# Layer-norm sums taken out of the residual additions and ScalarE squares, causal maxima by a fused VectorE instruction, rounding in one step, and new lists of the chains' order

## The reference

```python
x = x + L0_window_attention(layernorm(x))
x = x + L0_cross_attention(layernorm(x), ctx, ctx, mask)
x = x + L0_slots(layernorm(x))
x = x + L1_causal_attention(layernorm(x))      # softmax(q k / 4 + bias), bias holds the causal mask
x = x + L1_cross_attention(layernorm(x), ctx)
x = x + L1_mlp(layernorm(x))                   # quantized linear, depthwise conv, silu, quantized linear
```

## Time and profile before

| | |
|---|---|
| median of 3 executions | 3288.36 us (3285.29 to 3289.53) |
| the profiled execution | 3283.83 us, its span 3282.0 us |
| granted TensorE clock, mean of the span | 0.955 |
| PE busy (matmuls) | 2836.4 us, 86% |
| DVE (VectorE) busy | 2522.0 us, 77% |
| ACT (ScalarE) busy | 2178.7 us, 66% |
| POOL (GpSimd) busy | 755.3 us, 23% |
| DMA | 43.47 MB, mean 13 GB/s |

### The profile page before, as it was taken

The page is one execution under the profiler, slowest core; times in us unless marked ns, Lnnn a source line. Parts: engine busy times, 40 slices in busy tenths (PEclk is TensorE's granted clock), DMA queues, the critical chain, the costliest instruction groups (busy, mean ns, idle before and its releaser), DMA issues.

```text
span 3282.0 us, 59801 instructions
## 1 busy us (share of the span) xinstructions
PE 2836.4 (86%) x23406; PEld 2073.9 (63%) x23406; DVE 2522.0 (77%) x5446; ACT 2178.7 (66%) x4271; POOL 755.3 (23%) x1360
## 2 busy tenths in 40 slices
PE   3799986999878998899988998889988999889985
PEld 3566754676656766577666676567665676656763
DVE  6856599766898579975898769986799768987676
ACT  2368764678646876577855777657865687557773
POOL 1420013300233112330133112422032301232100
PEclk8799997999989999899999999999999999999996
DMA  5000010000000000000000000000000000000000
GB/s 157 1 1 1 4 27 17 1 1 5 24 12 9 1 16 12 20 1 1 16 21 11 1 4 13 24 9 1 5 24 12 9 1 16 16 17 1 1 1 13
DMA packets 43468, 43.47 MB, mean 13 GB/s; under 512 B 8577, under 2 KB 41185, under 8 KB 43185
## 3 DMA queue, kind: packets, MB, share of 16 engines
q1 hardware_dynamic: 41200, 36.46, 3.8%
q10 hardware_dynamic: 1984, 3.18, 0.3%
HBM read 31.24 MB, written 8.39 MB: 12 GB/s over the span
## 4 chain that ended last, share of the span: by engine, by line
PE 49%; DVE 31%; ACT 11%; POOL 4%; issue 4%; DMA 1%; SPq 0%; DVEq 0%; POOLq 0%; ACTq 0%
PE banks L1179 8%; PE banks L1213 7%; DVE chain_m L696 5%; PE banks L1322 4%; PE banks L1222 4%; PE banks L1260 4%; PE banks L1197 3%; DVE chain_arena L890 3%; PE banks L1286 2%; DVE chain_arena L927 2%; PE banks L1406 2%; DVE chain_arena L730 2%; DVE chain_arena L931 2%; DVE chain_stat L674 2%; DVE chain_arena L774 2%
## 5 line engine op out<-in xcount | busy, mean ns | idle before, releaser
L1213 PE MATMUL banks<-chain_arena 64*128 64x256 f32 x3072 | 426.2, 399 | 42.4 <-DVE chain_m L696 28.1
L696 DVE TENSOR_REDUCE chain_m<-banks 128x4 f32<-128x512 f32 x512 | 328.7, 681 | 84.8 <-PE banks L1213 84.2
L1515 POOL TENSOR_SCALAR chain_ng<-chain_sv 128x2 f32<-128x2 f32 x192 | 52.9, 276 | 1408.4 <-DVE chain_sv L677 1408.3
L1213 PEld LDWEIGHTS banks<-chain_arena 64*128 64x128 f32 x3072 | 286.0, 191 | 119.9 <-DVE chain_m L696 41.2
L1034 ACT ACTIVATE chain_arena<-chain_arena,chain_m 128x128 f32<-128x128 f32 x1024 | 324.1, 393 | 25.9 <-DVE chain_m L696 23.2
L968 ACT ACTIVATE chain_xn<-chain_xa,chain_nm,chain_rs 128x256 f32<-128x256 f32 x384 | 209.4, 596 | 166.3 <-POOL chain_nm L1519 165.5
L1260 PE MATMUL banks<-chain_arena 64*128 64x256 f32 x2048 | 268.2, 382 | 0.0
L692 DVE TENSOR_TENSOR chain_arena<-banks,pos_bias 128x512 f32<-128x512 f32 x256 | 174.9, 683 | 95.6 <-PE banks L1213 94.6
L1222 PE MATMUL banks<-chain_arena,chain_va 128*32 128x128 f32 x5120 | 198.1, 281 | 40.5 <-ACT chain_arena L1013 27.4
L1260 PEld LDWEIGHTS banks<-chain_arena 64*128 64x128 f32 x2048 | 200.5, 192 | 23.5
L1569 POOL TENSOR_TENSOR chain_arena<-chain_arena 128x512 f32<-128x512 f32 x128 | 169.5, 1341 | 148.4 <-DVE chain_arena L774 148.0
(11 more groups left out here) (314 smaller groups left out, 6979.1 us busy)
## 6 DMA issues: line engine op xcount, KB each, us to landing
chain_xn<-in_ctx SPq DMA_DIRECT2D x32, 256.0 KB, 2.8
chain_xa<-in_x SPq DMA_DIRECT2D x32, 256.0 KB, 3.1
out<-chain_xa SPq DMA_DIRECT2D x32, 256.0 KB, 2.2
chain_arena<-in_mask SPq DMA_DIRECT2D x32, 128.0 KB, 3.5
f_w1t<-in_w1t ACTq DMA_DIRECT2D x1, 1024.0 KB, 7.0
f_w2t<-in_w2t ACTq DMA_DIRECT2D x1, 1024.0 KB, 14.3
wqkv0T<-in_wqkv0T ACTq DMA_DIRECT2D x1, 768.0 KB, 16.8
whh<-in_whh SPq DMA_DIRECT2D x1, 768.0 KB, 10.3
```

Source lines behind the costliest of these rows:

```text
L696: e.tensor_reduce(m, s.rearrange("p (j o) t -> p j o t", o=2), AX.X, ALU.max, negate=True).then_inc(*done(f"{tag}_mx{u}"))
L1213: mm[i] = e.matmul(c.ps[:, i, 2 * T * j:2 * T * j + 2 * T], t["qh"][p, j, x, b, :], flat(t["kx"][p, j, b]), start=not masked, stop=not mas ...
```

## The change

The sums of the norms `b`, `f`, `1`, `x` and `g` no longer come from `bn_stats`. The residual addition before each becomes two `tensor_tensor_reduce` calls of 128x256 (`add_rows`), which also give the sum of each row. ScalarE turns it into the negated mean (128x2) and takes two `Square` activations of 128x256 with that mean as bias, whose accumulated output is the sum of squared differences. GpSimd makes variance plus epsilon from it, and the root and product as before. The norm `a`, of the input, stays as it was. In the causal attention each score tile takes four `tensor_tensor_reduce` calls of 128x128, which write `-(score + bias)` and the minimum of it, in place of one addition and one reduction; the exponential gets `scale=-1.0`. The hidden tile of the MLP is rounded by one VectorE instruction that adds and subtracts the constant. All lists of `ORDER` are new. The number of steps per turn falls from 85 to 80 on VectorE, rises from 81 to 84 on ScalarE, and stays on TensorE (92), GpSimd (17) and SyncE (2).

```diff
+def add_rows(e, c, tag, rows):
+    for b in range(B):
+        x = c.t["xa"][:, b, :]
+        y = e.tensor_tensor_reduce(x, rows(b), x, 1.0, 0.0, ALU.add, ALU.add, c.t["sm"][:, b:b + 1])
+    y.then_inc(*c.dve.now(f"{tag}_y"))
...
 def maxima_vector(e, c, n, tag, k, bias=False):
...
-            e.tensor_tensor(flat(t["s"][:, u % 4]), c.ps[:, u % 2, :], flat(k["pos_bias"][:, r]), ALU.add).then_inc(*done(f"{tag}_bi{u}"))
-            e.wait_ge(*dve(f"{tag}_bi{u}"))
-        s = t["s"][:, u % 4] if bias else bank(c, u % 2)
+            for a in range(PER):
+                mx = e.tensor_tensor_reduce(t["s"][:, u % 4, a], bank(c, u % 2)[:, a], k["pos_bias"][:, r, a // 2, a % 2], -1.0, 3e38, ALU.add, ALU.min,
+                                            max_of(t["m"], b, r, a))
+            mx.then_inc(*done(f"{tag}_mx{u}"))
+            yield
+            continue
+        s = bank(c, u % 2)
...
-    e.tensor_tensor(flat(t["xa"][:]), c.ps[:, 1, :], flat(t["xa"][:]), ALU.add).then_inc(*done(f"{tag}_y"))
+    add_rows(e, c, tag, lambda b: c.ps[:, 1, D * b:D * b + D])
...
-        e.wait_ge(*act(f"g_ro{b}"))
-        e.tensor_scalar(t["hq"][:, :, b, :], cv[:, :, b, :], -ROUND, None, ALU.add).then_inc(*done(f"g_r2{b}"))
+        e.wait_ge(*dve(f"g_mu{b}"))
+        e.tensor_scalar(t["hq"][:, :, b, :], cv[:, :, b, :], ROUND, -ROUND, ALU.add, ALU.add).then_inc(*done(f"g_r2{b}"))
...
-    yield from norm_vector(e, c, n, "b", "a_y")
-    yield from norm_vector(e, c, n, "f", "b_y")
-    yield from norm_vector(e, c, n, "1", "f_y")
-    yield from norm_vector(e, c, n, "x", "1_y")
-    yield from norm_vector(e, c, n, "g", "x_y")
...
-def norm_scalar(e, c, n, tag):
+def norm_scalar(e, c, n, tag, before=None):
+    if before:
+        e.wait_ge(*dve(f"{before}_y"))
+        e.activation(t["ng"][:], t["sm"][:], ACT.Copy, scale=-1.0 / D).then_inc(*done(f"{tag}_ng"))
+        e.wait_ge(*act(f"{tag}_ng"))
+        for b in range(B):
+            sq = e.activation(t["xn"][:, b, :], t["xa"][:, b, :], ACT.Square, bias=t["ng"][:, b:b + 1], accum_out=t["sq"][:, b:b + 1])
+        sq.then_inc(*done(f"{tag}_sq"))
+        yield
     e.wait_ge(*pool(f"{tag}_nm"))
...
-                ex = e.activation(s, s, ACT.Exp, bias=max_of(t["m"], u // GROUPS, row_group(u), a))
+                ex = e.activation(s, s, ACT.Exp, scale=-1.0, bias=max_of(t["m"], u // GROUPS, row_group(u), a))
...
-    for b in range(B):
-        v = t["cv"][:, :, b, :]
-        e.wait_ge(*dve(f"g_mu{b}"))
-        e.activation(v, v, ACT.Identity, bias=k["rounder"][:, 0:1]).then_inc(*done(f"g_ro{b}"))
...
 def norm_pool(e, c, n, tag, k):
+    else:
+        e.wait_ge(*act(f"{tag}_sq"))
+        e.tensor_scalar(t["rv"][:], t["sq"][:], 1.0 / D, LN_EPS, ALU.mult, ALU.add).then_inc(*done(f"{tag}_ve"))
+        e.wait_ge(*pool(f"{tag}_ve"))
```

Of the lists one line stands for all, the start of ScalarE's:

```diff
     "scalar": (
-        "301233030131230200313110223021122012333000121132233330303013...
+        "132011312312013033121223001302032021110133332102102102101331...
```

More of the change, by code:

```diff
@@ L100 @@
     "sync": (
[L101 removed]
+        "0011223313123020113322001133220011332200113322001133220011332200"),
     "pool": (
[L103 to L105 removed]
@@ new lines @@
+        "1320113322001320111133331120222300031202032103210320131321103320221110013333111122211323313323220200"
+        "1322012000300032012011130323311121022331113131013133300223232132222003021202000003021021031103233111"
+        "1201111223313103130033322321323222200102230200003020102103110323311112011112233131031300333223213232"
+        "2220010223020000302010210311032331111201111223313103130033322321323222200102230200003020102103110323"
+        "3111120111122331310313003332232132322220010223020000302010210311032331111201111223313103130033322321"
@@ L791, in window_vector @@
     e.wait_ge(*pe("a_pr"))
-    e.tensor_tensor(flat(t["xa"][:]), c.ps[:, 1, :], flat(t["xa"][:]), ALU.add).then_inc(*done("a_y"))
+    add_rows(e, c, "a", lambda b: c.ps[:, 1, D * b:D * b + D])
     yield
@@ L853, in slots_vector @@
     e.wait_ge(*pe("f_o"))
-    e.tensor_tensor(t["xa"][:], ps[:, :, 0:D], t["xa"][:], ALU.add).then_inc(*done("f_y"))
+    add_rows(e, c, "f", lambda b: ps[:, b, 0:D])
     yield
@@ L1075, in scalar_turn @@
     yield
-    yield from norm_scalar(e, c, n, "b")
+    yield from norm_scalar(e, c, n, "b", "a")
     e.wait_ge(*pe("b_T"))
@@ L1088, in scalar_turn @@
     yield from outputs_scalar(e, c, n, "b")
-    yield from norm_scalar(e, c, n, "f")
+    yield from norm_scalar(e, c, n, "f", "b")
     yield from normalized_scalar(e, c, n, "f", t["xnT"], 0)
@@ L1109, in scalar_turn @@
     yield
-    yield from norm_scalar(e, c, n, "1")
+    yield from norm_scalar(e, c, n, "1", "f")
     yield from normalized_scalar(e, c, n, "1", t["xnT"], 0)
@@ L1115, in scalar_turn @@
     yield from outputs_scalar(e, c, n, "1")
-    yield from norm_scalar(e, c, n, "x")
+    yield from norm_scalar(e, c, n, "x", "1")
     yield from normalized_scalar(e, c, n, "x", t["xnT"], 0)
@@ L1121, in scalar_turn @@
     yield from outputs_scalar(e, c, n, "x")
-    yield from norm_scalar(e, c, n, "g")
+    yield from norm_scalar(e, c, n, "g", "x")
     e.wait_ge(*dve("g_sc"))
@@ L1512, in norm_pool @@
 def norm_pool(e, c, n, tag, k):
-    t, dve, pool, done = c.t, c.dve.of(n), c.pool.of(n), c.pool.now
-    e.wait_ge(*dve(f"{tag}_mv1"))
-    e.tensor_scalar(t["ng"][:], t["sv"][:, :, 0], -1.0, None, ALU.mult).then_inc(*done(f"{tag}_ng"))
-    e.wait_ge(*dve(f"{tag}_ve"))
+    t, act, dve, pool, done = c.t, c.act.of(n), c.dve.of(n), c.pool.of(n), c.pool.now
+    if tag == "a":
+        e.wait_ge(*dve(f"{tag}_mv1"))
+        e.tensor_scalar(t["ng"][:], t["sv"][:, :, 0], -1.0, None, ALU.mult).then_inc(*done(f"{tag}_ng"))
+        e.wait_ge(*dve(f"{tag}_ve"))
+    else:
+        e.wait_ge(*act(f"{tag}_sq"))
+        e.tensor_scalar(t["rv"][:], t["sq"][:], 1.0 / D, LN_EPS, ALU.mult, ALU.add).then_inc(*done(f"{tag}_ve"))
+        e.wait_ge(*pool(f"{tag}_ve"))
     e.tensor_tensor(t["rs"][:], t["rv"][:], k["neg_half"][:], ALU.pow).then_inc(*done(f"{tag}_rs"))
```

213 lines of the change are left out of this document (101 added, 112 removed).

## The result

Slower: 3307.6 us, median of 4 runs (3304.1 to 3309.5), against 3289.0 for the kernel before on the same chip; ratio 1.0056, 95% interval 1.0039 to 1.0073. I had forecast 3261.

A forecast was written before the change was run, and what follows sets the result against it. No single engine bounds the kernel: VectorE sets the middle stretch of each 385.5 us period, TensorE the last. Terms -6.0 + 3.0 - 0.4 = -3.4 us per period, -27 in eight, took 3288.4 to 3261; range 3240 to 3282, chance 0.50.

The forecast's parts named there:

- +3.0 per period for ScalarE: First and last stretches of a period: ScalarE's free time falls from 56 to 41 us, lengthening TensorE's idle time by 3.
- The bounds reading: VectorE, 92% busy, sets the middle 142 us stretch; 7 norms saving 0.93 us each shorten it by 6.0 per period.
- VectorE's sum: VectorE's busy time over the run: norms -149 us, causal tiles +25, together -124 of 2522 (-233 to +153).
- the fused maxima give nothing: Causal tiles: four fused calls at 0.367 us make 1.47 against 1.37 now, +25 us over 256 tiles.
- ScalarE's sum: ScalarE's busy time: squares and means +206 us over 160 norms, 64 roundings gone -72, together +134 (to +200).
- Rounding: MLP hidden tile: the rounding chain without its ScalarE step gets shorter, counted as -0.4 us per period.
- I add nothing for the ends: Set-up, start and drain outside the eight periods (198 us): no change counted, though the lists differ there too.
- better lists: Rival: new lists mix the middle stretch with the others, cutting TensorE's idle time; -72 in all, 3216; chance 0.18.
- Half rate: Rival: the fused VectorE call's columns cost twice, 0.77 us per 256 and 0.50 per 128; +42, 3330; chance 0.08.
- The wash: Rival: ScalarE's extra visits in its strict list cancel the middle stretch's gain, within 6.6 us of 3288; chance 0.12.
- The longer way: Rival: norm path lengthens by 0.68 us, five times per turn, and sets the period; +34, 3322; chance 0.12.
- the three signs: Signs of error: 128-column call over 0.45 us, square much dearer than plain activation, ScalarE's product wait well above 166 us.

The follow-up runs named there:

- run 9: Kernel before, lists untouched, with a discarded negated mean and two squares on an always-ready tile added behind each of 160 pairs of normalized rows on ScalarE: 3426.4 us, +142.3.
- run 10: Kernel before plus one ScalarE turn per norm, a discarded 0.2 us instruction waiting for the residual addition; run 6 without its squares: 3345.8 us, +61.7.
- run 6: Kernel before with its own norm, plus ScalarE turns computing unused negated mean and squares, on the same ScalarE list as run 3: 3395.8 us, +109.8.
- run 5: Run 3 with each square over 8 of a row's 256 columns (variance not the reference's): 3345.3 us, +59.2 against the kernel before.
- run 3: Kernel before with the norm change alone, 160 turns put into ScalarE's list, 443 other turns shifted one to five places: 3376.3 us, +89.2.
- run 7: All three parts of the change, squares moved to the head of the normalized rows' turn, so no added turn and the order of before: 3598.8 us, +312.7.
- run 14: Kernel before, no instruction changed, lists searched anew: 3218.4 us, -65.7.
- run 15: Changed kernel, instructions unchanged, lists searched with the same effort as run 14: 3229.9 us, -54.2 against the kernel before.
- run 16: Kernel before on the lists of run 14, with only the causal tiles through the fused call: 3207.1 us, -78.7 against the kernel before.
- run 8: Changed kernel on its new lists with the old norm back and the added turns gone: 3349.0 us, +62.9 against the kernel before.
- run 12: Kernel before, no instruction touched, with run 3's ScalarE list minus the added turns (443 turns one to five places away): 3345.4 us, +57.0.
- run 18: Causal tiles and rounding as changed, norm as before, lists searched nearly twice as long as for run 15: 3169.2 us, -119.3 against the kernel before.

## Why the prediction was wrong

**The step that failed: +3.0 per period for ScalarE.** It let the squares lie in ScalarE's idle time, and made the price grow as that time shrinks. In the steady part TensorE's waits for ScalarE grew by 11.0 us per period and not by 3.0. Runs of its own bear it out: run 9 has +142 in all, some 18 per period, for 205 us of dead work with the lists untouched, and the squares alone are +48 (run 10 against 6). Busy 66% did not mean room. A microsecond of work on ScalarE came through at 0.3 to 0.7: 48 for 161 of busy time from run 10 to 6, 30 for 61 from run 5 to 3, 142 for 205 in run 9. What sets that factor was not isolated. That in a fixed order everything behind an instruction is late with it is argued from runs 7 and 9, where TensorE's waits for ScalarE grow by 190 and 109 us; a part comes through the granted clock, as the table shows.

**The bounds reading**, -6.0 per period, held that VectorE sets the middle stretch, so that work taken from it counts there almost in full. In the changed kernel TensorE's waits for VectorE fell by 7.7 per period, causal tiles included, so its size was about right there. It isn't a property of the instructions alone, as I took it to be: with the old lists the statistics of 160 norms came off VectorE and TensorE's waits for it stayed (226 and 228 us, runs 6 and 3). So the forecast -6.0 + 3.0 stands against -7.7 + 11.0, with 1.2 more for GpSimd, where I had put nothing, and 1.7 more of TensorE's busy time.

**Where the 19 us come from.** Runs 14 to 16 split them: with the lists of one search each, the changed instructions are 11.5 us slower (norm +24.5, causal tiles -13, rounding 0), and the new lists of the change stand 7 us further from what the search finds than the old ones (72.9 against 65.7). The norm's price was 25 to 37 with own lists, 32 in the steps on one list and 60 with the old list kept. It was a gain of 44 only on the lists made for it (run 8). The split between norm and lists is soft: it depends on two searches that need not be equally lucky, and a longer one moved run 15 by 24 us.

**VectorE's sum** was -124 us and is -283. I had put the read behind the call (0.082 more) and the call at its full length. Measured start to start, a call is 0.21 us at 128 columns (I took 0.367) and 0.34 at 256 (2028.27 to 2028.61; I took 0.50). A tile is 0.9, not 1.47. So "the fused maxima give nothing" was wrong by its price: they are what gains. The Trainium skill, "VectorE: DVE Perf Modes", section on two Vector instructions with no wait between them, says that an accumulator output is two instructions, and the trace agrees: 1024 reads beside 1024 calls. To add a time for the second was my step, and the timeline shows it covered by the next call.

**ScalarE's sum**, +134, is +109. The new instructions cost what I took: the squares with their reads are busy for 174.9 us, 0.547 each (I took 0.545), the means 32.9. The total grew by less than these make, since ScalarE's instructions overlap with their neighbours; I did not follow where. The size of the work was about right, its price in time was not.

**Rounding**, -0.4 per period: 0, within 6 us.

**"I add nothing for the ends"**: the steady part loses some 65 us and the rest gives some 45 back. I did not follow where in the ends.

**The lists.** I gave better lists 18 in 100 and no case to worse ones. Run 12 shows +57 from small shifts, runs 14 and 18 show 66 and more to be had. The order was the largest term of this kernel, and I had it only as a rival.

**The rivals and the signs.** Half rate is out. The wash is out: 18.7 is beyond 6.6. The longer way had the sign right, and as a mechanism it is not shown. The way grew, by 0.41 us at its shortest (I had said 0.68) and 0.87 in the mean, but the mean is as long with the old way kept (4.76 in run 6) and 4.47 with nothing changed but the list (run 12): so most of the lateness comes with ScalarE's order and load, and not with the longer chain of steps. The wait that I had named for it shrank. None of the three signs by which I wanted to know that I was wrong appeared (a call over 0.45 us, a dear square, a longer wait for the product). I had named none for plain work on ScalarE, which is what it was.

## What to carry to other kernels

Where several chains share engines in a fixed order, an engine's idle share is no room. Before moving work to the engine that everybody passes, try a dead copy of it there; it showed the sign here and overstated the size (142 us in run 9, 53 above its list in run 6, 25 to 37 for the norm change with own lists). Split TensorE's idle time by the engine it waits for, before and after: it told here in one table what the busy times did not. Moving work off the busier engine was worth less than its time, and less than what the receiver paid. When instructions change, compare each set with lists made for it by equal effort, and measure the list alone, since an order fitted to one set cost 44 us under another here (run 8).

## What the hardware showed unexpectedly

- VectorE's fused call with accumulated output: 286 ns each by the records, but 0.21 us start to start at 128x128, and its read (83 ns) starts together with the next call.
- ScalarE's accumulated square: 501 ns over 256 columns and 293 over 8; its read is recorded at 187 ns, and the second square starts 0.50 us after the first (2030.83), before the first one's read has ended (2031.24 and 0.19).
- An order in which 17% of one engine's turns stand one to five places away (443 of 2592) costs 1.7%, with no engine's instructions changed (2175 us on ScalarE in run 12, 2179 before).
- The same 23406 matmuls were busy for 2801 us (run 18) to 2956 us (run 7), at mean granted clocks of 0.962 and 0.929. Of run 7's 313 us, 120 are this.
